# Flamingo gated block with a 2:4-sparse FFN: the down projection's weight parts are split in every step instead of read back from DRAM, and the last rows are added by VectorE

## The chip, the cores and the metric
One Trainium2 chip (trn2), one NeuronCore of it. The metric is the device time of one execution in microseconds, the median of the runs of a kernel. Lower is better.

## The reference
Inputs are x (32, 128, 512), a context of the same shape, a mask over the context's rows and two gates; the FFN's weights are w_gate and w_up (512, 2048) and w_down (2048, 512), all float32.

```python
x = x + tanh(g_xattn[0]) * xattn(layernorm(x), ctx, mask)     # softmax(q ctx^T / sqrt(512)) ctx, masked
h = silu(xn @ w_gate) * (xn @ w_up)                           # xn = layernorm(x)
h = h, with the two smaller of each four neighbours by |h| set to 0
x = x + tanh(g_ffn[0]) * (h @ w_down)
```

## The kernel before, in words
**Stages.** The first 155 us or so are attention, one batch after the other, which stores x1 to the output and the normalised x1, transposed, to a scratch tensor in DRAM (xnT). The rest is the FFN, over 4096 rows in PAIRS = 4 pairs of 1024 rows, each pair in QS = 4 quarters of the 2048 inner columns: STEPS = 16 steps `s`. A step has two units `u = 2s` and `2s + 1`, each a quarter's half of the inner columns for both halves of the pair's rows.

**Precision.** Every float32 matrix that TensorE reads is held as two fp32r parts: a high part (ScalarE copies the value to fp32r) and a low part (value less high part, by VectorE, or by POOL for w_down). A product is three matmuls: high by high, high by low, low by high.

**A unit on TensorE** (`product`, L983 to L1023): seven products (a Strassen-like form of the two-by-two block product of gate, up and the two row halves), each twice (e = 0, 1) of six matmuls, 84 in all. Product k = 4 waits for ScalarE's copy_a1 (a1_copied), k = 5 for copy_d0, k = 6 for VectorE's add_c22 (c22), k = 0 of the next unit for gated0. After the products of unit u come the down tiles of step `u // 2 - 1`, row half `u % 2` (`down`, L1069): four tiles t of 12 matmuls into two PSUM banks ps_y in turn. So half 0 of step s runs behind the products of unit 2s + 2, half 1 behind those of 2s + 3, and both halves of step 15 at the very end, with no products before them. A tile waits for the copy of the tile two before it (y_copied) and, its first, for the parts of h and of w_down.

**Hidden tiles.** For each step and row half, ScalarE makes |h| of four tiles (h_abs, in the place of h_hi), VectorE makes six compares (L849), a counting block of five instructions in bf16 (L857 to L864) and four keeps (L875); then ScalarE makes the high parts (L626) and VectorE the low parts (L882). h_abs lies over h_hi, so |h| of one half waits for the down tiles of the step before to be done.

**The down parts.** `dn` holds both parts of one quarter (2 MB over 128 partitions). Steps 0 to 3 build them: SP loads 1 MB of raw values into dn[:, 1] (L382) from a contiguous scratch copy of w_down (one 4 MB DRAM to DRAM copy, L433), ScalarE makes four high parts (L630, in unit 2s + 2, after copy_d0), POOL four low parts in place (L531), and SP stores the 2 MB to dn_scratch (L391). The quarters run to and fro (0 1 2 3, 3 2 1 0, ...), so steps 4, 8 and 12 find their parts still there; the other nine steps from 5 on reload 2 MB (L386). A load waits until the down tiles of the step before are all done, since they read the same dn.

**Weights and x.** Units 1 to 7 build their gate and up weights as units run: SP loads four raw pieces (L245), ScalarE spreads each (L261) and makes seven high parts (L273), VectorE four sums and seven low parts (L277 to L294), SP stores them (L365); later units reload them into w_ring (L372). The x parts of the next pair are made in the same way, two a unit at most, through x_blk and x_out (L311, L316 to L332, L355).

**Order of the work.** Each engine runs one list, written out by hand, and waits only at its own semaphores. On ScalarE, in the even unit: |h|, copy_a0, four h high parts, two SiLUs, two copy_a1, an x high part, spread 0, copy_d0, spread 1, copy_d0, dn high parts, w high part 0, spread 2, two h high parts, two SiLUs, w high part 1, spread 3, then the four copies of y (L640) with w high parts between them. On SP, in the odd unit of steps 0 to 2: w pieces, an x store (which waits for VectorE's x low part), w stores, the second x store, the raw load of dn, five w stores. POOL adds y to the output by accumulating DMAs (L536), four a half.

**End.** After unit 31: tiles of step 14's half 1, then ScalarE's h high parts and |h| of half 1, VectorE's h low parts, six compares, counting, keeps; the tiles of step 15's two halves; for each tile a copy by ScalarE (L640) and an adding DMA by POOL.

## Time and profile before
| | |
|---|---|
| median of 3 runs | 1163.98 us (1161.43 to 1169.27) |
| the profiled execution | 1164.87 us, its span 1163.1 us |
| TensorE matmul busy | 1091.0 us, 94% |
| VectorE, ScalarE, POOL busy | 790.7, 605.8, 230.7 us (68, 52, 20%) |
| mean granted TensorE clock | 0.982 |
| HBM read, written | 168.82 MB, 114.29 MB |

How to read it: PE is TensorE, DVE VectorE, ACT ScalarE, POOL GpSimd, SP SyncE (it issues DMAs). Matmul durations overlap (0.39 us each at a start every 0.23), so starts say more than busy shares. A gap's cause stands behind it in brackets, with its length in us. A row with x2 or more merges instructions that follow each other; its start is the first one's.

### The profile page before, as it was taken

How to read it: one execution, taken by the hardware profiler on the slowest of the kernel's cores; microseconds unless marked ns; L12 is line 12 of the kernel's file. 1: busy time of each engine (PE TensorE's matmuls, PEld its weight loads, DVE VectorE, ACT ScalarE, POOL GpSimd, SP SyncE). 2: the span in 40 equal slices, each digit the busy share in tenths (PEclk: the TensorE clock that was granted, in tenths of full speed). 3: DMA queues.
4: the chain of work that ended last, by engine and by line, in shares of the span. 5: the costliest groups of instructions: out<-in, count | busy, mean ns of one | idle time of the engine just before them, and what ended most of it. 6: DMA issues, size and time to landing. Idle time of an engine off the chain costs nothing.

```text
span 1163.1 us, 15073 instructions
## 1 busy us (share of the span) xinstructions
PE 1091.0 (94%) x4960; PEld 888.9 (76%) x4960; DVE 790.7 (68%) x1365; ACT 605.8 (52%) x1092; POOL 230.7 (20%) x413
## 2 busy tenths in 40 slices
PE   6988888799998999999999999999999999999967
PEld 5766566587776878888888788888888888888846
DVE  6999847969697676666675667575847373747480
ACT  6988556567675444444444445444544344444432
POOL 5767300313122131111110011011011111111112
PEclk9999898999999999999999999999999999999989
DMA  7999586798989997788789877887888766778445
GB/s 261 349 382 340 189 285 222 290 344 270 323 251 296 370 304 191 190 237 257 192 261 299 279 195 199 228 270 199 270 274 255 159 161 152 230 158 221 94 109 72
DMA packets 94078, 279.92 MB, mean 241 GB/s; under 512 B 9200, under 2 KB 9200, under 8 KB 89072
## 3 DMA queue, kind: packets, MB, share of 16 engines
q1 hardware_dynamic: 75568, 245.40, 59.3%
q0 software_dynamic: 18432, 33.56, 21.6%
q8 instruction: 40, 0.66, 0.2%
q14 instruction: 38, 0.31, 0.1%
HBM read 168.82 MB, written 114.29 MB: 243 GB/s over the span
## 4 chain that ended last, share of the span: by engine, by line
PE 70%; DVE 13%; DMA 9%; issue 3%; ACT 3%; SPq 1%; POOL 1%; POOLq 0%; ACTq 0%; DVEq 0%
PE ps_y L1086 9%; PE ps_y L1088 9%; PE ps_y L1087 9%; PE ps_a L1017 8%; PE ps_a L1021 8%; PE ps_a L1019 8%; PE ps_d L1017 4%; PE ps_d L1019 4%; PE ps_d L1021 4%; DMA x_blk<-xnT_scratch 3%; PE ps_c L1021 2%; PE ps_c L1017 2%; PE ps_c L1019 2%; DMA w_raw<-in_L_ffn_w_up 2%; DVE beats L849 2%
## 5 line engine op out<-in xcount | busy, mean ns | idle before, releaser
L536 POOL DMA_DIRECT2D out_rows<-y_out x128 | 110.7, 865 | 768.9 <-ACT y_out L640 741.5
L1086 PE MATMUL ps_y<-dn,h_hi 128*128 128x512 f32 x512 | 203.6, 398 | 24.6 <-DMA dn<-dn_scratch 11.4
L1017 PE MATMUL ps_a<-xm,w_ring 128*128 128x512 f32 x512 | 203.2, 397 | 15.3 <-DVE w_ring L277 7.3
L1019 PE MATMUL ps_a<-xm,w_ring 128*128 128x512 f32 x512 | 202.4, 395 | 0.0
L1021 PE MATMUL ps_a<-xm,w_ring 128*128 128x512 f32 x512 | 202.4, 395 | 0.0
L1088 PE MATMUL ps_y<-dn,h_lo 128*128 128x512 f32 x512 | 202.0, 395 | 0.0
L1087 PE MATMUL ps_y<-dn,h_hi 128*128 128x512 f32 x512 | 201.7, 394 | 0.0
L640 ACT ACTIVATE y_out<-ps_y,ffn_gate 128x512 f32<-128x512 f32 x128 | 88.0, 688 | 199.4 <-PE ps_y L1088 199.4
L817 DVE TENSOR_TENSOR cp<-ps_c,cp 128x512 f32<-128x512 f32 x64 | 43.9, 691 | 150.7 <-PE ps_c L1021 150.7
L1086 PEld LDWEIGHTS ps_y<-dn,h_hi 128*128 128x128 f32 x512 | 97.5, 190 | 49.0 <-DMA dn<-dn_scratch 11.8
L1017 PEld LDWEIGHTS ps_a<-xm,w_ring 128*128 128x128 f32 x512 | 97.6, 191 | 38.1 <-issue 9.5
L849 DVE TENSOR_TENSOR beats<-h_abs 128x512 bf16<-128x512 f32 x192 | 120.3, 686 | 1.4 <-ACT h_abs L621 1.3
L626 ACT ACTIVATE h_hi<-hidden 128x512 fp32r<-128x512 f32 x128 | 73.3, 625 | 79.2 <-DVE hidden L875 79.2
L1021 PEld LDWEIGHTS ps_a<-xm,w_ring 128*128 128x128 f32 x512 | 97.8, 191 | 20.8
L1088 PEld LDWEIGHTS ps_y<-dn,h_lo 128*128 128x128 f32 x512 | 97.6, 191 | 21.0
L1019 PEld LDWEIGHTS ps_a<-xm,w_ring 128*128 128x128 f32 x512 | 97.8, 191 | 20.6
L1087 PEld LDWEIGHTS ps_y<-dn,h_hi 128*128 128x128 f32 x512 | 97.7, 191 | 20.5
L1017 PE MATMUL ps_d<-xm,w_ring 128*128 128x512 f32 x256 | 100.1, 391 | 1.9 <-ACT hidden L607 1.9
L1019 PE MATMUL ps_d<-xm,w_ring 128*128 128x512 f32 x256 | 99.9, 390 | 0.0
L1021 PE MATMUL ps_d<-xm,w_ring 128*128 128x512 f32 x256 | 99.7, 390 | 0.0
L882 DVE TENSOR_TENSOR h_lo<-hidden,h_hi 128x512 fp32r<-128x512 f32 x128 | 81.1, 684 | 14.0 <-ACT h_hi L626 14.0
L621 ACT ACTIVATE h_abs<-hidden 128x512 f32<-128x512 f32 x128 | 76.2, 625 | 27.6 <-DVE hidden L841 27.6
(91 smaller groups left out, 1750.5 us busy)
## 6 DMA issues: line engine op xcount, KB each, us to landing
w_ring<-w_scratch SPq DMA_DIRECT2D x147, 512.0 KB, 4.6
out_rows<-y_out POOLq DMA_DIRECT2D x128, 256.0 KB, 4.1
w_scratch<-w_ring SPq DMA_DIRECT2D x56, 512.0 KB, 8.1
xm_scratch<-x_out SPq DMA_DIRECT2D x42, 512.0 KB, 5.2
xm<-xm_scratch SPq DMA_DIRECT2D x21, 1024.0 KB, 7.0
dn<-dn_scratch SPq DMA_DIRECT2D x9, 2048.0 KB, 11.1
x_in<-in_x SPq DMA_DIRECT2D x32, 256.0 KB, 6.3
ctx_in<-in_ctx SPq DMA_DIRECT2D x32, 256.0 KB, 6.4
```

The lines of the kernel that those rows point to most:

```text
L536: nc.gpsimd.dma_start(out[RING * ((s - 1) // QS) + TILES * ORDER[order] + n % TILES], y_out[:, n % 4], accum_op=ALU.add).then_inc(y_stored ...
L621: nc.scalar.activation(h_abs[:, h, j], hidden[:, h, j], ACT.Abs).then_inc(abs_done, 1)
L626: nc.scalar.activation(h_hi[:, h, j], hidden[:, h, j], ACT.Copy).then_inc(h_hi_done, 1)
L640: nc.scalar.activation(y_out[:, n % 4], ps_y[n % 2][:], ACT.Identity, scale=ffn_gate[:]).then_inc(y_copied, 1)
L849: nc.vector.tensor_tensor(beats[:, PAIR[i, j]], h_abs[:, h, i], h_abs[:, h, j], ALU.is_ge).then_inc(beats_done, 1)
L882: nc.vector.tensor_tensor(h_lo[:, h, j], hidden[:, h, j], h_hi[:, h, j].bitcast(F32), ALU.subtract).then_inc(h_lo_done, 1)
L1017: nc.tensor.matmul(to, w_ring[:, k, e, 0, c], xm[:, k, 0, c], start=begins and c == 0, stop=False, skip_group_check=not begins)
L1019: nc.tensor.matmul(to, w_ring[:, k, e, 0, c], xm[:, k, 1, c], start=False, stop=False, skip_group_check=not begins)
L1021: last = nc.tensor.matmul(to, w_ring[:, k, e, 1, c], xm[:, k, 0, c], start=False, stop=c == 1, skip_group_check=not begins)
L1086: nc.tensor.matmul(to, h_hi[:, h, j, at], dn[:, 0, j], start=at_j == 0, stop=False)
L1087: nc.tensor.matmul(to, h_hi[:, h, j, at], dn[:, 1, j], start=False, stop=False)
L1088: last = nc.tensor.matmul(to, h_lo[:, h, j, at], dn[:, 0, j], start=False, stop=at_j == GROUP - 1)
```

## The change
- dn_scratch, its stores and its reloads are gone. `DN_BUILT` lists the 13 steps that split: 0 to 3 and the nine that reloaded. From step 5 on, SP loads 1 MB of raw values straight from w_down into `w_raw`, whose use for gate and up is over by then, as soon as the split before is done (it no longer waits for the down tiles); for step 15 it does so in unit 30.
- ScalarE's high parts move forward: the first before copy_a1(0), the second before copy_a1(1), the others behind it. They wait for the raw part, and to write dn for the down tiles of the step before. POOL makes the low parts of all 13 steps.
- Step 15's parts go to `dn_last`, a place over xm that is free once product 1 of unit 31 is made; ScalarE makes the high parts behind copy_a1 of unit 31.
- |h| of step 15's half 1 goes to x_blk, so it waits for no down tile; VectorE puts two of its compares ahead of half 0's low parts.
- The last half's four tiles: SP loads these rows of the output (with all earlier additions in them) into `rows`, VectorE adds gate times ps_y to them, and SP stores them plainly. The last four y copies and accumulating DMAs are gone.
- w_down's scratch copy is made in four DMAs of 1 MB, one a step. The low parts 4 to 6 of the weights built in even units move on VectorE behind the two c11 additions of the odd unit.

```diff
+LAST = STEPS - 1
+DN_BUILT = [s for s in range(STEPS) if s < QS or s % QS]
...
+        sb = Place(0)
+        dn_last = sb("dn_last", [P, 2, GROUP, D], F32R, 4)
+        rows = sb("rows", [P, TILES, D], F32, 4)
...
+        def dn_places(s, j):
+            if s < QS:
+                return dn[:, 1, j].bitcast(F32), dn[:, 0, j], dn[:, 1, j]
+            to = dn_last if s == LAST else dn
+            return w_raw[:, j // 2, j % 2], to[:, 0, j], to[:, 1, j]
+        def abs_of(s, order):
+            return x_blk if (s, order) == (LAST, 1) else h_abs[:, ORDER[order]]
...
             def load_dn(s):
-                wait(sp, y_done, 2 * TILES * s)
                 if s < QS:
-                    if s == 0:
-                        sp.wait_ge(down_copied, 16)
-                    else:
-                        sp.wait_ge(dn_stored, 16 * s)
+                    wait(sp, y_done, 2 * TILES * s)
+                    wait(sp, dn_lo_done, GROUP * s)
+                    sp.wait_ge(down_copied, 16 * (s + 1))
                     sp.dma_start(dn[:, 1].rearrange("p j n -> p (j n)").bitcast(F32), raw_dram[s]).then_inc(dn_raw_loaded, 16)
                 else:
-                    if s == DN_RELOADED[0]:
-                        sp.wait_ge(dn_stored, 16 * QS)
-                    sp.dma_start(dn[:].rearrange("p h j n -> p (h j n)").bitcast(F32), dn_dram[weights_of(2 * s) // 2]
-                                 ).then_inc(dn_loaded, 16)
+                    sp.wait_ge(spread_done, 4 * BUILT)
+                    sp.wait_ge(dn_lo_done, GROUP * DN_BUILT.index(s))
+                    sp.dma_start(w_raw[:].rearrange("p a b n -> p (a b n)"), down_view[weights_of(2 * s) // 2]
+                                 ).then_inc(dn_raw_loaded, 16)
...
-                        if half == 0 and s > 0:
-                            store_dn(s - 1)
+                        if half == 0:
+                            if s + 1 < QS:
+                                sp.wait_ge(down_copied, 16 * (s + 1))
+                                copy_down(s + 1)
...
-                        if half == 1 and (s < QS or s in DN_RELOADED):
+                        if half == 1 and s in DN_BUILT and s != LAST:
+                            load_dn(s)
+                        if half == 0 and s == LAST:
                             load_dn(s)
...
+            b = B - RING + TILES * ORDER[1]
+            sp.dma_start(rows[:], out.rearrange("b s d -> s b d")[:, b:b + TILES]).then_inc(rows_loaded, 16)
+            for t in range(TILES):
+                sp.wait_ge(y_added, t + 1)
+                sp.dma_start(out[b + t], rows[:, t]).then_inc(rows_stored, 16)
...
+            for s in range(STEPS):
+                if s in DN_BUILT and s != LAST:
+                    dn_low(s)
+                for t in range(TILES):
+                    add_y(2 * TILES * s + t)
+                if s == LAST - 1:
+                    dn_low(LAST)
+                if s != LAST:
+                    for t in range(TILES, 2 * TILES):
+                        add_y(2 * TILES * s + t)
...
+            def dn_high(s, j):
+                raw, high, low = dn_places(s, j)
+                at = DN_BUILT.index(s)
+                act.wait_ge(dn_raw_loaded, 16 * (at + 1))
+                if s == LAST:
+                    act.wait_ge(made[1], 2 * UNITS)
+                else:
+                    wait(act, y_done, 2 * TILES * s)
+                nc.scalar.activation(high, raw, ACT.Copy).then_inc(dn_hi_done, 1)
...
                 silu0(u, 0)
                 silu0(u, 1)
+                if s - 1 in DN_BUILT:
+                    dn_high(s - 1, 0)
                 copy_a1(u, 0)
+                if s - 1 in DN_BUILT:
+                    dn_high(s - 1, 1)
                 copy_a1(u, 1)
+                if s - 1 in DN_BUILT:
+                    dn_high(s - 1, 2)
+                    dn_high(s - 1, 3)
                 x_high_at(s, 0)
...
-                if 0 < s <= QS:
-                    for j in range(GROUP):
-                        dn_high(s - 1, j)
...
+            compare(s, 1, ((0, 1), (2, 3)))
             for j in kept_order(s):
                 h_low(s, 0, j)
-            compare(s, 1, ((0, 1),) + REST + ((2, 3),))
+            compare(s, 1, REST)
...
+            for t in range(TILES):
+                n = TILES * (2 * LAST + 1) + t
+                dve.wait_ge(y_done, n + 1)
+                if t == 0:
+                    dve.wait_ge(rows_loaded, 16)
+                nc.vector.scalar_tensor_tensor(rows[:, t], ps_y[n % 2][:], ffn_gate[:], rows[:, t], ALU.mult,
+                                               ALU.add).then_inc(y_added, 1)
...
-                if s < QS:
-                    pe.wait_ge(dn_lo_done, GROUP * (s + 1))
-                elif s in DN_RELOADED:
-                    pe.wait_ge(dn_loaded, 16 * (DN_RELOADED.index(s) + 1))
+                if s in DN_BUILT:
+                    pe.wait_ge(dn_lo_done, GROUP * (DN_BUILT.index(s) + 1))
+                right = dn_last if s == LAST else dn
```

## Rows read from the trace of the kernel before
**Rows 1.** The stage table, 520 to 640 us: us, engines' busy us, clock, DMA, GB/s
```profile
520.00:640.00 120.00, 120.00 (x530) 99.25 (x529) 76.89 (x126) 55.06 (x94) 13.86 (x17) 1.00 0.86 254
```

**Rows 2.** The waits of TensorE, whole span: us in total, times, longest
```profile
PE ps_y L1086 <- DMA dn<-dn_scratch: 11.4, 1, 11.4
...
PE ps_y L1086 <- POOL dn L531: 8.6, 4, 2.7
...
PE ps_y L1086 <- ACT y_out L640: 4.5, 3, 2.2
...
PE ps_d L1017 <- ACT hidden L607: 1.9, 1, 1.9
```

**Rows 3.** Timeline of TensorE in the tail: start, us, engine, line
```profile
1131.96 0.80 PE L1086 MATMUL ps_y<-dn,h_hi 128*128 128x512 f32 x1 [11.39 <-DMA dn<-dn_scratch]
...
1138.01 0.39 PE L1088 MATMUL ps_y<-dn,h_lo 128*128 128x512 f32 x1
```

**Rows 4.** Timeline of VectorE, then ScalarE and POOL, in the tail
```profile
1118.84 0.68 DVE L875 SCALAR_TENSOR_TENSOR hidden<-part,hidden 128x512 f32<-128x512 bf16 x1
...
1124.45 3.70 DVE L849 TENSOR_TENSOR beats<-h_abs 128x512 bf16<-128x512 f32 x6
...
1128.18 0.42 DVE L857 TENSOR_TENSOR part<-beats 128x512 bf16<-128x512 bf16 x1
...
1130.91 0.69 DVE L875 SCALAR_TENSOR_TENSOR hidden<-part,hidden 128x512 f32<-128x512 bf16 x1
...
1157.09 0.69 ACT L640 ACTIVATE y_out<-ps_y,ffn_gate 128x512 f32<-128x512 f32 x1 [2.03 <-PE ps_y L1088]
...
1158.07 0.86 POOL L536 DMA_DIRECT2D out_rows<-y_out  x1 [1.85 <-ACT y_out L640]
```

**Rows 5.** DMA issues: count, KB each, median us to landing; last row L416, 256 KB each
```profile
out_rows<-y_out POOLq DMA_DIRECT2D x128, 256.0 KB, 4.1
...
dn<-down_scratch SPq DMA_DIRECT2D x4, 1024.0 KB, 7.0
...
w_raw<-in_L_ffn_w_up SPq DMA_DIRECT2D x16, 512.0 KB, 7.6
...
DMA to landing us min/median/max: 2.0/5.5/9.8
```

**Rows 6.** Timelines of SyncE, ScalarE, VectorE and TensorE around step 1's splitting
```profile
271.13 0.53 SPq L382 DMA_DIRECT2D dn<-down_scratch  x1
...
276.69 1.89 SPq L245 DMA_DIRECT2D w_raw<-in_L_ffn_w_up  x2
...
274.04 1.07 ACT L601 ACTIVATE cp<-ps_a 128x512 f32<-128x512 f32 x2
...
286.14 1.14 ACT L261 ACTIVATE w_blk<-w_raw 128x512 f32<-128x512 f32 x1 [4.88 <-DMA w_raw<-in_L_ffn_w_up]
...
293.04 0.68 DVE L283 TENSOR_TENSOR w_blk<-w_blk 128x512 f32<-128x512 f32 x1
...
297.59 0.50 PE L1086 MATMUL ps_y<-dn,h_hi 128*128 128x512 f32 x1 [1.04 <-ACT y_out L640]
```

**Rows 7.** POOL's low parts and VectorE beside them, steps 1 and 2
```profile
279.26 7.19 POOL L531 TENSOR_TENSOR dn<-dn 128x512 fp32r<-128x512 f32 x4 [12.85 <-ACT dn L630]
...
280.00 1.28 DVE L823 TENSOR_TENSOR hidden<-ps_a,hidden 128x512 f32<-128x512 f32 x2
...
281.98 1.67 DVE L860 TENSOR_TENSOR beats<-beats 128x1024 bf16<-128x1024 bf16 x1
...
346.25 0.69 DVE L332 TENSOR_TENSOR x_blk<-x_blk 128x512 f32<-128x512 f32 x1
...
L531 POOL TENSOR_TENSOR dn<-dn x1: 2566/2566/2566, 345.5 to 345.5; 128x512 fp32r<-128x512 f32 x1
```

**Rows 8.** ScalarE and VectorE in unit 14, whose products begin at 578.45
```profile
585.03 1.14 ACT L611 ACTIVATE cp<-cp 128x512 f32<-128x512 f32 x2
...
591.96 1.28 DVE L823 TENSOR_TENSOR hidden<-ps_a,hidden 128x512 f32<-128x512 f32 x2
```

More of the change, by code:

```diff
@@ L89 @@
 RELOADED = [u for u in range(BUILT, UNITS) if u % BUILT]
-DN_RELOADED = [s for s in range(QS, STEPS) if s % QS]
+LAST = STEPS - 1
+DN_BUILT = [s for s in range(STEPS) if s < QS or s % QS]
 def wait(engine, semaphore, value):
@@ L526, in _, with dn_low, add_y @@
                 pool.wait_ge(x1_stored[k], 16 * (B // 4))
[L527 to L537 removed]
+            def dn_low(s):
+                for j in range(GROUP):
+                    raw, high, low = dn_places(s, j)
+                    pool.wait_ge(dn_hi_done, GROUP * DN_BUILT.index(s) + j + 1)
+                    nc.gpsimd.tensor_tensor(low, raw, high.bitcast(F32), ALU.subtract).then_inc(dn_lo_done, 1)
+            def add_y(n):
+                order = n // TILES % 2
+                pool.wait_ge(y_copied, n + 1)
+                nc.gpsimd.dma_start(out[RING * (n // (2 * TILES * QS)) + TILES * ORDER[order] + n % TILES], y_out[:, n % 4],
+                                    accum_op=ALU.add).then_inc(y_stored[n % 4], 16)
+            for s in range(STEPS):
[8 more added lines that the diff above has]
+                        add_y(2 * TILES * s + t)
         @block.scalar
@@ L678, in _ @@
                 copy_d0(u, 1)
-                if 0 < s <= QS:
-                    for j in range(GROUP):
-                        dn_high(s - 1, j)
                 if building:
@@ L716, in _ @@
                 copy_a1(u, 1)
+                if s == LAST:
+                    for j in range(GROUP):
+                        dn_high(s, j)
                 x_high_at(s, 2)
@@ L733, in _ @@
                     absolute(s, 0, j)
+                if s == LAST:
+                    for j in range(GROUP):
+                        absolute(s, 1, j)
+                    for t, tiles in enumerate(((), kept_order(s)[:1], kept_order(s)[1:], ())):
+                        copy_y(s - 1, 1, t)
+                        for j in tiles:
+                            h_high(s, 0, j)
+                    break
                 for t in range(TILES):
@@ L741, in _ @@
                         x_high_at(s, 3)
-            for j in kept_order(STEPS - 1):
-                h_high(STEPS - 1, 0, j)
-            for j in range(GROUP):
-                absolute(STEPS - 1, 1, j)
-            for t in range(TILES):
-                copy_y(STEPS - 1, 0, t)
-                h_high(STEPS - 1, 1, kept_order(STEPS - 1)[t])
-            for t in range(TILES):
-                copy_y(STEPS - 1, 1, t)
+            for t, tiles in enumerate(((), kept_order(LAST)[:1], kept_order(LAST)[1:], ())):
+                copy_y(LAST, 0, t)
+                for j in tiles:
+                    h_high(LAST, 1, j)
         @block.vector
@@ L848, in compare @@
                     wait(dve, kept_done, GROUP * hs)
-                    nc.vector.tensor_tensor(beats[:, PAIR[i, j]], h_abs[:, h, i], h_abs[:, h, j],
+                    nc.vector.tensor_tensor(beats[:, PAIR[i, j]], abs_of(s, order)[:, i], abs_of(s, order)[:, j],
                                             ALU.is_ge).then_inc(beats_done, 1)
@@ L926, in _ @@
                     w_sum(dve, u + 1, 3)
-                    for k in range(2, PROD):
+                    for k in range(2, 4):
                         w_low(dve, nc.vector, u + 1, k)
@@ L936, in _ @@
                 add_c11(u, 1)
+                if u < BUILT:
+                    for k in range(4, PROD):
+                        w_low(dve, nc.vector, u, k)
                 if s > 0:
@@ L975, in _ @@
                 h_low(s, 1, j)
+            for t in range(TILES):
+                n = TILES * (2 * LAST + 1) + t
[4 more added lines that the diff above has]
+                                               ALU.add).then_inc(y_added, 1)
         @block.tensor
```

56 lines of the change are left out of this document (26 added, 30 removed).

## The prediction

> **What bounds the kernel now.** I read the page first, then the stage table, the waits of TensorE, the timelines of one splitting step, one later step and the tail, and the landing times of the DMAs. In 520 to 640 us TensorE starts 530 matmuls in 120 us, one per 0.226 us, with no idle time and the full granted clock [rows 1]. So in the feed-forward part TensorE is the bound, and a part of the change counts only where it makes or removes a gap there. The gaps that it touches are four kinds [rows 2]: one of 11.4 us for the reload of the down parts (the last step); four for POOL's low parts of steps 0 to 3, 8.6 us together; three for y_out, 4.5 us, at tile 3 of the down tiles of steps 0 to 2; one of 1.9 us behind a late ScalarE copy. The other eight reloads of dn never hold TensorE.
>
> Below, T is the start of the products of an even unit. A unit's products are 84 matmuls (19.0 us), a half's down tiles 48 (10.9 us); product 4 is due at T+10.9, product 6 at T+16.3, the down tiles at T+19.1.
>
> **The last step, where the gain is.** Now the tiles of step 14 are issued until 1120.6, TensorE waits 11.39 us for the 2 MB reload, which may start only then, and resumes at 1131.96 at 0.43 us per matmul, half the pace; at 1138.01 it is back at 0.23 [rows 3]. That is 13 slow matmuls, 2.7 us more. After the change the parts lie in dn_last, split during unit 31, so only the hidden tiles can hold TensorE. VectorE ends its keeps at 1119.5 [rows 4], makes two compares (0.60 each, from 3.70 for six), and the first low part is ready at 1121.4: a gap of 0.8 instead of 11.4. Half 1's tiles run 1121.4 to 1132.3. Meanwhile VectorE needs three more low parts, four compares (2.4), the counting (2.7, from 1128.18 to 1130.91), four keeps (2.4): done at 1130.8. High and low parts follow at 0.6 a tile, the first at 1131.4, so the second half starts at 1132.3 without a wait and is issued by 1143.2. Before, its last tile was handed to ScalarE at 1157.09 [rows 4]; now to VectorE at 1143.4. Gain 13.7.
> After it, before: 0.69 copy, 0.86 issue on POOL at 1158.07, 4.1 us of adding DMA [rows 4, 5], end 1163.1, in all 6.0. Now: one add of 0.7, an issue of 0.5, a plain 256 KB store. Such stores took 2.0 to 9.8, median 5.5, when the queues were full [rows 5]; here nothing else is moving, so I take 2.5, range 2.0 to 4.1: 3.8 in all, gain 2.2. The rows' load (1 MB) can start when the last add of step 14 has landed, near 1126, and with about 7 us it is there by 1133, before tile 0 is due at 1135. Below nothing: an add that takes long would stop tile 2; bound 3 us. Tail: -15.9, range -12 to -17.
>
> **Steps 0 to 2.** Here ScalarE now makes high part 0 before copy_a1, and waits for the raw part. SP still issues that load behind the x store: 271.13, and 1 MB takes 7.0 (6.8 to 7.8 in four), so it lands at 278.1 [rows 5, 6]. ScalarE starts copy_a1 at 274.04 now [rows 6]. So it stands still for some 4 us, product 4 waits 3.7 us, and what is queued behind it (x high part, spread 0, copy_d0) moves: four high parts of 0.52 and the wait add up to 6.1 us. Spread 0's end releases SP's load of the w_up piece, at 276.69 now, at 282.8 then, and ScalarE stands before spread 2 until it lands, at 286.14 now, 9.4 us after its issue, because five w stores were queued ahead. Later the queue is emptier: between 5 and the median of 7.6 [rows 5] it lands at 288.0 to 290.5. From there spread 2, two high parts of h, two SiLUs, w high and spread 3 (5.3 us, at 1.1 a spread and 0.5 to 0.6 the others) lead to VectorE's w_sum, at 293.04 now, and this over w_high to the second copy_y, for which tile 3 waits until 297.59 now [rows 6]. That chain, not TensorE, sets the step; TensorE's 3.7 us and the half clock after it are hidden in the wait for y_out. On VectorE's side now three counting instructions are stretched by POOL, 1.67 in place of 0.69 [rows 7], some 3 us; they come free because POOL starts sooner, but c22 waits for copy_d0 by as much. So w_sum starts at 294.3 (VectorE's own chain) to 295.8 (290.5 and 5.3). Net for step 1: +1.3 to +2.8. The same working with issues at 203.76 and 336.77 gives +0.6 to +1.8 for step 0 and 0 to +1.7 for step 2. Together +4.1, range 0 to +6.3. Step 3's raw part lands at 405 as ScalarE comes to it; POOL starts 5 us sooner and its 0.9 us gap goes. The smaller copies of w_down cost nothing (four of 1 MB for one of 4 MB; store_dn leaves the same queue). Moving three w_low on VectorE by half a unit fits the time in which it waits for product 1. Sum +3.2.
>
> **The eight later split steps.** ScalarE's wait is nearly nil: its SiLUs end at T+7.6 (585.03 and 1.14, T = 578.45) [rows 8], the raw load goes at about T+0.3 and takes 7; in steps 7, 13 and 14 it goes far earlier. Four high parts push copy_d0 by 2.1 us, to T+12.4; product 5 wants it at T+13.6. Cost nothing; without that cover it would be what the load is late beyond 1.2 us.
> POOL is the question. Alone its subtraction takes 1.3; one took 2.57 because it started at 345.5 under x_low and x_sum, and could not begin until 346.94 [rows 7]. VectorE, running without a gap, passed from one to the other and kept POOL out though POOL had been waiting 0.7 us. In these steps POOL is ready near T+8.5, inside four h_low and six compares without a gap, so I take it that it gets in where VectorE's first operation with a PSUM input begins, c22: at T+13.5 where there is an x_sum (591.96) [rows 8]. From c22 to POOL's end is the 6.45 us of step 1 (280.0 to 286.45) [rows 7], so the low parts are ready at T+19.95: a gap of 0.9, in two steps; in the other six c22 or the gap before it comes 0.6 to 1.1 us sooner, and the parts are in time, with 0.2 each in three of them for a copy_y made late by VectorE's 3 us of counting. +2.4. In return the reload no longer stands before the x block at 639, and the 1.9 us gap at 654 [rows 2] goes. Sum +0.5, range -2 to +12.
> The Trainium skill, "SBUF — State Buffer", section "Who interferes with whom", says that a VectorE instruction with two SBUF inputs contends with a GpSimd one that reads SBUF, that the lock is exclusive and held for an instruction, and that issue order decides. The stretched rows agree; how a waiting POOL stands against a stream of VectorE no sentence there tells, and it is the first rival.
>
> **Sum.** -15.9 + 3.2 + 0.5 = -12.2. The profiled execution took 1164.87 (span 1163.1), 0.9 above the median of 1163.98, so the forecast is 1151.8 for the median.
>
> **Rivals.**
> 1. POOL wins each handover, slower than before. For it: in step 1 the three counting instructions alternate with POOL's [rows 7]; against it: 346.25. Each subtraction then puts 1.07 us (1.67 less 0.60) into VectorE's stream before c22, 4.3 in all. c22 was done at T+14.2 with x_sum, 13.6 with x_low, 13.0 without; it decides once it is later than T+16.3. Gaps 2.2 in two steps, 1.6 in three, 1.0 in three: 12.2, less 1.9, and step 3 loses 1.5 rather than gains 0.9. In steps 0 to 2 it takes the upper end, 6.3. +18.1 - 15.9 = +2.2: 1166.2.
> 2. The raw parts of steps 0 to 2 land before ScalarE wants them, and it does not stand. The splits start 5 us sooner, c22 is free of POOL, VectorE's chain is up to 1.5 us shorter in each step: -4.5 for +4.1, so 1143.2. Against it: load and SiLU both follow VectorE, 3 us apart in all three steps, and the load takes 7.
> 3. The end gives less: the rows land late or a hidden tile holds the second half, and with a gap near 3 us the clock falls again. +4: 1155.8.
>
> **How the numbers follow.** Forecast 0.52, rival 1 0.2, rival 2 0.1, rival 3 0.18. The forecast's own range is 1147 to 1158. The range 1145 to 1166 leaves out most of rival 2, half of rival 1 and little else. A measurement of this kernel tells about 1% from no change; the border is 1152.3. Faster by over 1%: half of the forecast and rival 2 and a little of 3, 0.42; slower by over 1% needs rival 1 with more, 0.05; within, 0.53.
>
> **What would show it.** Right: no wait on a dn load; a gap near 1 us at the first down tile of step 15 and the full clock there; ScalarE standing some 3 to 4 us before the first high part in steps 0 to 2, a gap at product 4, w_up issued 6 us later; POOL's four subtractions of the later steps ending near T+20 with the first stretched to 4 us or more. Wrong: gaps before product 6 (POOL broke the stream), no wait for the raw part, or a last tile handed over later than 1146 less the earlier shift.

## The result and the profile after

The changed kernel takes 1161.47 us (median of 12 runs, 1158.17 to 1163.88), the kernel before 1165.47 beside it (12 runs, 1161.43 to 1169.27): ratio 0.9964, 95% interval 0.9949 to 0.9979. So it is faster, by 0.36%; the medians are 4.0 us apart, about a third of the 12.2 us of the forecast. The profiled executions are 1 us apart in span, 1163.1 and 1162.1: the one of the changed kernel is the slowest of its 12 runs (1163.88).

The waits of TensorE in the changed kernel's profile (us in total, times, longest), for [rows 2]:

```profile
PE ps_a L1084 <- ACT cp L636: 15.2, 4, 6.9
PE ps_a L1084 <- DVE hidden L879: 13.6, 9, 2.2
...
PE ps_y L1155 <- ACT y_out L686: 3.5, 3, 1.6
...
PE ps_y L1155 <- DVE h_lo L938: 1.1, 1, 1.1
```

The 11.4 us on the reload of dn and the 8.6 us on POOL's parts are gone, as is the 1.9 us behind a late ScalarE copy. In their place stand 13.6 us on `hidden` of L879. That is c22, the addition that frees the PSUM bank of product 4 for product 6. One of these nine waits is in unit 8 (1.24 us), eight are in units 12 to 30. Three of the four waits of the first line, 11.5 us, stand before product 4 in steps 0 to 2; the fourth is at the start of the FFN, as before. The stage table for the stretch of [rows 1], 520 to 640 us:

```profile
520.00:640.00 120.00, 116.15 (x503) 95.19 (x502) 81.56 (x120) 56.81 (x100) 25.67 (x22) 0.99 0.79 233
```

It had 530 starts of matmuls and no idle time, and has 503. The timeline of TensorE there, at product 6 of unit 14:

```profile
599.68 0.47 PE L1084 MATMUL ps_a<-xm,w_ring 128*128 128x512 f32 x1 [2.22 <-DVE hidden L879]
...
600.74 0.63 PE L1086 MATMUL ps_a<-xm,w_ring 128*128 128x512 f32 x1
601.16 0.63 PE L1088 MATMUL ps_a<-xm,w_ring 128*128 128x512 f32 x1
...
603.72 0.54 PE L1088 MATMUL ps_a<-xm,w_ring 128*128 128x512 f32 x1
604.10 0.39 PE L1155 MATMUL ps_y<-dn,h_hi 128*128 128x512 f32 x1
```

Behind the gap eight matmuls start 0.43 us apart, half the pace, 1.6 us more. What came late shows on ScalarE, VectorE and POOL in the same unit (its products start at 580.95, the T of the prediction):

```profile
587.22 2.49 DVE L938 TENSOR_TENSOR h_lo<-hidden,h_hi 128x512 fp32r<-128x512 f32 x4
...
589.02 0.64 ACT L676 ACTIVATE dn<-w_raw 128x512 fp32r<-128x512 f32 x1 [0.37 <-DMA w_raw<-in_L_ffn_w_down]
...
589.63 8.09 DVE L905 TENSOR_TENSOR beats<-h_abs 128x512 bf16<-128x512 f32 x6
...
589.74 6.84 POOL L555 TENSOR_TENSOR dn<-w_raw,dn 128x512 fp32r<-128x512 f32 x4 [6.75 <-ACT dn L676]
...
598.85 1.28 DVE L879 TENSOR_TENSOR hidden<-ps_a,hidden 128x512 f32<-128x512 f32 x2
```

The six compares take 8.09 us instead of 3.70 [rows 4]. POOL's four subtractions, ready 0.1 us after the first compare started, take 6.84 where the four of the last step, with VectorE mostly idle beside them, take 5.06. They alternate with VectorE's: the first compare takes 0.69 us, the next four 1.78 each. c22 comes at T+17.9 instead of T+13.5 [rows 8], and product 6 was due at T+16.3. The sizes of the compares one by one (source view of L905, 589 to 598 us):

```profile
L905 DVE TENSOR_TENSOR beats<-h_abs x6: 678/1776/1784, 589.6 to 597.0; 128x512 bf16<-128x512 f32 x6
```

**Where the microsecond comes from.** Four stretches, cut at rows that both profiles have: up to the first gap of the FFN, 154.52 before and 156.40 after, +1.9, attention (in the profiles of the runs below, with the same attention code, this point lies anywhere from 152.9 to 156.4); from there to tile 3 of step 2 (364.46 and 364.39), -1.9; from there to the end of step 14's tiles (1120.6 and 1135.1), +14.6; from there to the end, 42.5 and 27.0, -15.5. Together -1.0 before rounding. The tail gave what was forecast, and the steps between took it back.

### The profile page after: what moved, and what is told of

Its sections match the earlier page's. It is cut to its first block, busy times and chain, and to the rows that moved or that the text cites. A ratio compares the mean times of both kernels' runs of the same rounds, so it can differ in the third digit from the quotient of the medians.

```text
span 1162.1 us, 15204 instructions
## 1 busy us (share of the span) xinstructions
PE 1093.2 (94%) x4960; PEld 889.3 (77%) x4960; DVE 822.3 (71%) x1369; ACT 619.5 (53%) x1124; POOL 285.0 (25%) x445
## 4 chain that ended last, share of the span: by engine, by line
PE 64%; DVE 18%; DMA 8%; issue 5%; ACT 3%; SPq 1%; POOL 0%; DVEq 0%; ACTq 0%; POOLq 0%
PE ps_y L1155 8%; PE ps_y L1157 8%; PE ps_y L1156 8%; PE ps_a L1084 8%; PE ps_a L1086 7%; PE ps_a L1088 7%; DVE beats L905 5%; PE ps_d L1088 3%; PE ps_d L1086 3%; PE ps_d L1084 3%; PE ps_c L1088 2%; PE ps_c L1086 2%; PE ps_c L1084 2%; DMA x_blk<-xnT_scratch 2%; DMA dn<-down_scratch 2%
## 5 line engine op out<-in xcount | busy, mean ns | idle before, releaser
L560 POOL DMA_DIRECT2D out_rows<-y_out x124 | 107.4, 866 | 655.4 <-ACT y_out L686 629.5
L1084 PE MATMUL ps_a<-xm,w_ring 128*128 128x512 f32 x512 | 206.3, 403 | 35.1 <-ACT cp L636 15.2
L1086 PE MATMUL ps_a<-xm,w_ring 128*128 128x512 f32 x512 | 204.9, 400 | 0.0
L1088 PE MATMUL ps_a<-xm,w_ring 128*128 128x512 f32 x512 | 204.4, 399 | 0.0
L1155 PE MATMUL ps_y<-dn,h_hi 128*128 128x512 f32 x480 | 187.5, 391 | 3.5 <-ACT y_out L686 3.5
L1157 PE MATMUL ps_y<-dn,h_lo 128*128 128x512 f32 x480 | 187.2, 390 | 0.0
L1156 PE MATMUL ps_y<-dn,h_hi 128*128 128x512 f32 x480 | 186.7, 389 | 0.0
L686 ACT ACTIVATE y_out<-ps_y,ffn_gate 128x512 f32<-128x512 f32 x124 | 85.1, 687 | 165.3 <-PE ps_y L1157 165.2
L905 DVE TENSOR_TENSOR beats<-h_abs 128x512 bf16<-128x512 f32 x186 | 156.2, 897 | 1.5 <-ACT h_abs L659 1.5
L1084 PEld LDWEIGHTS ps_a<-xm,w_ring 128*128 128x128 f32 x512 | 98.8, 193 | 61.9 <-issue 33.9
L1088 PEld LDWEIGHTS ps_a<-xm,w_ring 128*128 128x128 f32 x512 | 99.3, 194 | 21.6
L1086 PEld LDWEIGHTS ps_a<-xm,w_ring 128*128 128x128 f32 x512 | 99.1, 194 | 20.7
L1155 PEld LDWEIGHTS ps_y<-dn,h_hi 128*128 128x128 f32 x480 | 90.2, 188 | 23.4 <-ACT y_out L686 4.7
L1157 PEld LDWEIGHTS ps_y<-dn,h_lo 128*128 128x128 f32 x480 | 90.1, 188 | 19.3
L1156 PEld LDWEIGHTS ps_y<-dn,h_hi 128*128 128x128 f32 x480 | 90.1, 188 | 19.1
L879 DVE TENSOR_TENSOR hidden<-ps_a,hidden 128x512 f32<-128x512 f32 x64 | 42.9, 686 | 58.9 <-PE ps_a L1088 56.9
```

The costliest lines, as they stand in the source:

```text
L560: nc.gpsimd.dma_start(out[RING * (n // (2 * TILES * QS)) + TILES * ORDER[order] + n % TILES], y_out[:, n % 4], accum_op=ALU.add).then_inc( ...
L686: nc.scalar.activation(y_out[:, n % 4], ps_y[n % 2][:], ACT.Identity, scale=ffn_gate[:]).then_inc(y_copied, 1)
L905: nc.vector.tensor_tensor(beats[:, PAIR[i, j]], abs_of(s, order)[:, i], abs_of(s, order)[:, j], ALU.is_ge).then_inc(beats_done, 1)
L1084: nc.tensor.matmul(to, w_ring[:, k, e, 0, c], xm[:, k, 0, c], start=begins and c == 0, stop=False, skip_group_check=not begins)
L1086: nc.tensor.matmul(to, w_ring[:, k, e, 0, c], xm[:, k, 1, c], start=False, stop=False, skip_group_check=not begins)
L1088: last = nc.tensor.matmul(to, w_ring[:, k, e, 1, c], xm[:, k, 0, c], start=False, stop=c == 1, skip_group_check=not begins)
```

## The experiments

Each run has its own runs of the kernel before beside it: 1164.88 us in runs 1 to 4, 1165.62 in 5 to 8, 1166.77 in 9 to 12. The ratios are to these.

**1. The tail alone.** Steps 5 to 14 store and reload both parts as before; steps 0 to 3 split early as changed.

```diff
-DN_BUILT = [s for s in range(STEPS) if s < QS or s % QS]
+DN_BUILT = [0, 1, 2, 3, LAST]
+DN_RELOADED = [s for s in range(QS, LAST) if s % QS]
...
+                        if half == 0 and s > 0:
+                            store_dn(s - 1)
```

> The changed kernel, but steps 5 to 14 reload both parts from a DRAM copy as before (the copy and its stores are back); the first steps, step 15 and the end are as changed. Theory (POOL's subtractions, reading SBUF, break VectorE's stream before c22 and so hold product 6): no gap at product 6 in the later steps, the 1.9 us gap at 654 is back, and the time is 12.4 us of gaps and some 2 of half clock below the changed kernel, so near 1147 to 1149. Rival (the end gave less than its 15.6 us, and the later steps cost little): the time stays within 3 us of the changed kernel, near 1160.

1156.87 us, ratio 0.9935 (0.9914 to 0.9956). The gaps at product 6 of the later steps are gone, but for one of 1.4 us in unit 8, the tail is as in the changed kernel, and the 1.8 us behind a late ScalarE copy is back. It missed by 8 us or more, and its profile has them in steps 1 and 2: tile 3 of step 2 starts 217.3 us after the first gap, against 209.9 before and 208.0 after. Run 10 takes this up.

**2. POOL writes and does not read** in steps 5 to 14. The low parts' values are left out, so this is a measurement and no kernel.

```diff
-                    nc.gpsimd.tensor_tensor(low, raw, high.bitcast(F32), ALU.subtract).then_inc(dn_lo_done, 1)
+                    if QS <= s < LAST:
+                        nc.gpsimd.memset(low.bitcast(F32), 0.0).then_inc(dn_lo_done, 1)
+                    else:
+                        nc.gpsimd.tensor_tensor(low, raw, high.bitcast(F32), ALU.subtract).then_inc(dn_lo_done, 1)
```

> In steps 5 to 14 POOL fills the low parts with zeros (it writes and reads nothing; the low part of w_down is left out there), ScalarE's high parts and the loads stay. Theory (the reads of POOL and VectorE meet): VectorE's six compares take 3.7 us again instead of 8.1, no gap at product 6, near 1147. Rival A (ScalarE's four high parts make copy_d0 and so c22 late): the gaps of 1.0 to 2.2 us stay, near 1161. Rival B (any POOL work on SBUF stops VectorE): the compares stay stretched, gaps as long as the fills are.

1148.37 us, ratio 0.9856 (0.9816 to 0.9895); no gap at product 6 from step 5 on. ScalarE's four copies, SP's loads and POOL's four waits are all still there. What is gone is POOL's reading, and with it some length: a fill takes 0.53 us, a subtraction 1.3. Run 11 takes these two apart.

**3. VectorE makes the low parts of steps 5 to 14**, behind c22.

```diff
+                if s - 1 >= QS and s - 1 in DN_BUILT:
+                    for j in range(GROUP):
+                        raw, high, low = dn_places(s - 1, j)
+                        dve.wait_ge(dn_hi_done, GROUP * DN_BUILT.index(s - 1) + j + 1)
+                        nc.vector.tensor_tensor(low, raw, high.bitcast(F32), ALU.subtract).then_inc(dn_lo_done, 1)
```

> In steps 5 to 14 VectorE makes the four low parts itself, behind the two c22 additions, 4 times 0.6 us. Theory: compares at 3.7 us, c22 in time, low parts ready 2.4 us after c22 at T+17.2 (due T+19.1), so no gap at product 6 nor at the first down tile, at most 0.3 us at a later tile: near 1147. Rival A (ScalarE late): gaps at product 6 stay, near 1161. Rival C (VectorE has no 2.4 us to give behind c22): gaps move to tile 2 of the down tiles, 1 to 2 us in eight steps, near 1158.

1146.66 us, ratio 0.9845 (0.9804 to 0.9886), and one gap, of 0.5 us, between unit 8 and the tail. With 2.5 us of work more on VectorE in each of eight steps the kernel is some 15 us faster than with that work on POOL.

**4. The same splits, half a step earlier**: raw load in the even unit, high parts ahead of the unit's SiLUs, POOL's subtractions in VectorE's idle time.

```diff
-                        if half == 1 and s in DN_BUILT and s != LAST:
+                        if half == 1 and s < QS:
                             load_dn(s)
-                        if half == 0 and s == LAST:
+                        if half == 0 and s > QS and s in DN_BUILT:
                             load_dn(s)
...
+                        if t == 2 * TILES - 1 and QS <= s + 1 < LAST and s + 1 in DN_BUILT:
+                            dn_low(s + 1)
```

> In steps 5 to 14 the raw part is loaded half a step earlier, ScalarE makes the four high parts first thing in the even unit and POOL starts at about T+1.5 while VectorE waits for product 1; POOL still subtracts. Theory: POOL's four take 1.3 us each and end near T+6.8, only the last one meets VectorE's low parts of h, no gap at product 6: near 1147. Rival A (ScalarE's 2.1 us make its chain late wherever they stand): copy_a0 late by 2, gaps at product 2 or 6 in each of the eight steps, 1158 or more.

1147.00 us, ratio 0.9841 (0.9793 to 0.9889). Its stage table shows TensorE full again, as [rows 1], with VectorE as busy as there (77.0 us for 76.9; 81.6 in the changed kernel):

```profile
520.00:640.00 120.00, 120.00 (x530) 99.18 (x529) 77.01 (x126) 58.38 (x103) 23.85 (x24) 1.00 0.84 245
```

**5. High parts of steps 0 to 3 at their old place**, all else as changed.

```diff
-                if s - 1 in DN_BUILT:
+                if s - 1 in DN_BUILT and s > QS:
                     dn_high(s - 1, 0)
...
+                if 0 < s <= QS:
+                    for j in range(GROUP):
+                        dn_high(s - 1, j)
```

> The changed kernel with the high parts of steps 0 to 3 put back behind the copies of product 3, where the kernel before had them; steps 5 to 14 stay as changed. Theory 1 (the one on record, that the early place costs time because ScalarE stands before the copies of product 2 until the raw rows have landed): the gaps of 6.91, 2.32 and 2.29 us at product 4 go (11.5 us), those of the kernel before at the first down tile come back (2.32, 2.67, 2.68 and about 0.9, together 8.6 us), and the copies' own 3.5 us of the first step stays: the time falls by 0 to 4 us, best value 1159. Theory 2 (the two places are worth the same within a microsecond, because the time that the early place takes from the copies it gives back at the first down tile): 1161 to 1162, and step 2's last tile starts within 1 us of 364.4 us less the shift of the start. The eight gaps at product 6 stay in both, 12.4 us together.

1160.25 us, ratio 0.9946 (0.9925 to 0.9967); the changed kernel's 0.9949 to 0.9979 overlaps. From the first gap to tile 3 of step 2 it takes 207.9 us, the changed kernel 208.0. Theory 2: the place is worth nothing that these runs resolve. Of the 11.5 us of gaps before product 4, 2.9 stay; the gaps at the down tiles of steps 0 to 2 grow from 3.5 to 11.6.

**6 and 12. POOL kept out until c22**, once by a wait for the second of the two additions (run 6, below), once for the first (run 12, `c22_done[0]`). Run 6 was meant to wait for the first, and its expectation says so, but `c22_done[1]` counts the second; run 12 is what that expectation describes.

```diff
             def dn_low(s):
+                if QS <= s < LAST:
+                    pool.wait_ge(c22_done[1], 2 * (s + 1) + 1)
```

> The changed kernel with one wait more: in steps 5 to 14 POOL begins its four subtractions only when VectorE has done the first addition of product 4's results, so that it cannot enter VectorE's unbroken run of compares. This is the order that the prediction on record took for granted. Theory 1 (POOL's reads of SBUF inside that run make product 6 late): the gaps at product 6 go (12.4 us) with the half clock behind two of them (some 3.5 us), gaps of at most about 1 us at the first down tile take their place in the five steps whose stream has an x_sum; 1146 to 1152 us, best value 1149. Theory 2 (the gaps come from ScalarE's four copies ahead of product 2's copies): the gaps stay as they are, 1161 us.

> As the run in which POOL waits for product 4's additions, but for the first of the two instead of the second: POOL may start some 0.64 us sooner, where the prediction let it in. That run had gaps of 1.63 (six) and 2.4 us (two) at the first down tile, 14.7 together, as POOL's four subtractions took 6.2 us against VectorE's counting. Theory (the end of POOL's four, not their start's neighbour, sets the gap): each gap shrinks by 0.6, 9.7 us together, and the run takes 1159.5, range 1157 to 1162. By the prediction on record the gaps would be 0.9 in two steps and nil in the others, 1151 us.

Run 6: 1164.48 us, ratio 0.9999 (0.9979 to 1.0019). Run 12: 1151.70 us, ratio 0.9883 (0.9854 to 0.9912). I had expected 1146 to 1152 of run 6 and 1157 to 1162 of run 12; it was the other way round. TensorE's waits, run 6, then run 12:

```profile
PE ps_a L1086 <- ACT cp L638: 15.3, 4, 6.8
PE ps_y L1157 <- POOL dn L557: 14.7, 8, 2.5
```

```profile
PE ps_y L1157 <- POOL dn L557: 3.0, 5, 0.9
...
PE ps_a L1086 <- DVE hidden L881: 1.4, 1, 1.4
```

In both, the eight gaps at product 6 are gone and others stand at the first down tile, 14.7 us or 3.0. The timelines of unit 14 say why (run 6, then run 12):

```profile
592.77 1.28 DVE L881 TENSOR_TENSOR hidden<-ps_a,hidden 128x512 f32<-128x512 f32 x2
...
594.14 6.19 POOL L557 TENSOR_TENSOR dn<-w_raw,dn 128x512 fp32r<-128x512 f32 x4 [13.39 <-DVE hidden L881]
...
600.38 0.50 PE L1157 MATMUL ps_y<-dn,h_hi 128*128 128x512 f32 x1 [2.42 <-POOL dn L557]
```

```profile
585.71 3.70 DVE L907 TENSOR_TENSOR beats<-h_abs 128x512 bf16<-128x512 f32 x6
...
590.53 1.29 DVE L881 TENSOR_TENSOR hidden<-ps_a,hidden 128x512 f32<-128x512 f32 x2
...
591.30 5.83 POOL L557 TENSOR_TENSOR dn<-w_raw,dn 128x512 fp32r<-128x512 f32 x4 [12.22 <-DVE hidden L881]
...
597.19 0.50 PE L1157 MATMUL ps_y<-dn,h_hi 128*128 128x512 f32 x1 [0.93 <-POOL dn L557]
```

Run 12's POOL begins under the second addition, which reads one of its inputs from PSUM and is not stretched, and its last subtraction ends 6.60 us after c22 began. Run 6's begins 1.37 us after c22 began instead of 0.77, meets four counting instructions that are stretched in full instead of three, and ends 7.56 after it. With the tiles due 5.2 to 5.7 us after c22 begins, that is a gap of 2.4 or of 0.9. In the six other steps the parts are in time or up to 0.5 us late in run 12, and 1.6 late in run 6.

**7. The last rows as in the kernel before**, by ScalarE's copy and POOL's adding DMA.

```diff
-            for t in range(TILES):
-                n = TILES * (2 * LAST + 1) + t
-                dve.wait_ge(y_done, n + 1)
-                if t == 0:
-                    dve.wait_ge(rows_loaded, 16)
-                nc.vector.scalar_tensor_tensor(rows[:, t], ps_y[n % 2][:], ffn_gate[:], rows[:, t], ALU.mult,
-                                               ALU.add).then_inc(y_added, 1)
+            for t in range(TILES):
+                copy_y(LAST, 1, t)
```

> The changed kernel with the last four row tiles written as in the kernel before: ScalarE scales them out of PSUM into y_out and POOL adds each to the output by an accumulating DMA; VectorE's four adds, the load of 1 MB and the plain stores are left out. The step of the prediction that stands to be tested: the end behind TensorE's last matmul was to become 2.2 us shorter, by 0.9 us that is the fall from a landing of 4.1 to one of about 2.0 us and the rest from the missing hop through POOL. By it this run takes 1163.5 us. Rival: the end is set elsewhere and the run takes 1161.5 us, the same.

1164.12 us, ratio 0.9989 (0.9971 to 1.0007), 2.65 above the changed kernel. The intervals of the two overlap, but their profiles bear it out: from the first matmul of the last tiles to the end of the span it takes 28.88 us, the changed kernel 25.93.

This run's profile shows one thing more. In unit 12 there is no gap at product 6, where the changed kernel has 1.63 us. POOL's first subtraction came there during the third compare instead of the first, and was kept out of all the rest:

```profile
526.02 3.70 DVE L896 TENSOR_TENSOR beats<-h_abs 128x512 bf16<-128x512 f32 x6
...
527.61 7.94 POOL L545 TENSOR_TENSOR dn<-w_raw,dn 128x512 fp32r<-128x512 f32 x4 [8.22 <-ACT dn L665]
```

That first subtraction takes 3.27 us, and the six compares their 3.70. With the same instructions, c22 is in time when POOL does not get in between.

**8. Runs 4 and 5 together**, the splits of steps 5 to 14 early and the high parts of steps 0 to 3 late.

```diff
+                if s - 1 >= QS and s - 1 in DN_BUILT:
+                    for j in range(GROUP):
+                        dn_high(s - 1, j)
                 silu0(u, 0)
...
                 copy_d0(u, 1)
+                if 0 < s <= QS:
+                    for j in range(GROUP):
+                        dn_high(s - 1, j)
```

> The kernel in which the splits of steps 5 to 14 are made in the step before, ahead of VectorE's run (147.0 us over a thousand in the last series), with the high parts of steps 0 to 3 at the place of the kernel before. If the two act apart from each other: 1147.0 us less what the first run of this series gains over the changed kernel, so 1144 to 1147, best value 1145. If the gaps in steps 0 to 3 hide something of each other it does not fall below 1147.

1145.47 us, ratio 0.983 (0.9802 to 0.9859), the best value of the expectation. Since run 5's own gain of 1.2 us is within the noise, and so are the 1.5 us to run 4, this does not show that the two act apart from each other. It is the lowest of the kernels that leave nothing out, though runs 3, 4 and 9 can't be told from it.

**9. All low parts on VectorE**, with the high parts of steps 0 to 3 late.

```diff
+                if 0 < s <= QS:
+                    for j in range(GROUP):
+                        raw, high, low = dn_places(s - 1, j)
+                        dve.wait_ge(dn_hi_done, GROUP * DN_BUILT.index(s - 1) + j + 1)
+                        nc.vector.tensor_tensor(low, raw, high.bitcast(F32), ALU.subtract).then_inc(dn_lo_done, 1)
                 add_c12(u, 0)
```

> All subtractions of steps 0 to 14 on VectorE: those of steps 5 to 14 behind the additions of product 4, as in the run that took 1146.66 us, those of steps 0 to 3 behind the first two keeps, with the high parts of steps 0 to 3 at the place of the kernel before. In the run with early and late parts the first down tiles of steps 0 to 3 still waited 2.68, 1.46, 2.55 and 1.12 us for POOL (7.8 us). If POOL and VectorE hinder each other there too, VectorE's counting loses its stretch (some 3 us a step), the four subtractions cost it 2.5 us, and those gaps go: 1138 to 1143 us, best value 1141. If VectorE's own chain up to the sums for the next weights sets these steps anyway, as the gaps at tile 3 say, nothing is gained: 1145 to 1147.

1146.04 us, ratio 0.9836 (0.9809 to 0.9864): nothing gained. The counting is unstretched, but the low parts come after it, and the gaps at the down tiles are 3.47, 2.50, 3.85 and 1.86 us, 11.7 in all where run 8 has 7.8, while those for y_out fall from 5.4 to 0.7.

**10. As run 1, with the high parts of steps 0 to 3 at their old place.**

```diff
-                if s - 1 in DN_BUILT:
-                    dn_high(s - 1, 0)
                 copy_a1(u, 0)
...
                 copy_d0(u, 1)
+                if 0 < s <= QS:
+                    for j in range(GROUP):
+                        dn_high(s - 1, j)
```

> The tail of the change alone (reload from the scratch copy in steps 5 to 14, as before), with the high parts of steps 0 to 3 back at their old place. The run of the tail alone, with the high parts early, took 1156.87 us: its last tile of step 2 started 217.3 us after the first product's gap, where the kernel before has 209.9. Theory: the early place costs these 7 us, and only because the 2 MB store stands in SP's queue ahead of what ScalarE then waits for. By it this run takes 1149.5 us, range 1147 to 1151, and no gap over 4 us stands in 200 to 400. Rival: the order of SP's queue alone costs them: 1156 to 1158, as that run.

1157.09 us, ratio 0.9918 (0.9889 to 0.9946): the same as run 1, the rival. So the early place is not what slows steps 1 and 2. ScalarE's waits for the w_up piece, 200 to 400 us, in run 10, in the kernel before, in the changed kernel and in run 5:

```profile
ACT w_blk L279 <- DMA w_raw<-in_L_ffn_w_up: 31.5, 5, 9.1
```

```profile
ACT w_blk L261 <- DMA w_raw<-in_L_ffn_w_up: 24.2, 5, 5.3
```

```profile
ACT w_blk L276 <- DMA w_raw<-in_L_ffn_w_up: 12.1, 5, 3.6
```

```profile
ACT w_blk L276 <- DMA w_raw<-in_L_ffn_w_up: 20.4, 5, 5.5
```

The median landing of these pieces in that stretch is 9.3, 8.8, 5.4 and 8.6 us after the issue. It goes with the place of the high parts and not with the 2 MB store: late in run 5, without the store, it is 8.6; early in run 1, with the store, it is 5.1.

The store does cost time here. In these steps run 10 differs from run 5, and run 1 from the changed kernel, by the 2 MB store of the parts and by the raw load that waits for it. From the first gap to tile 3 of step 2 run 10 takes 216.8 us for run 5's 207.9, and run 1 217.3 for 208.0: 9 us both times. The kernel before has the store too and takes 209.9, but makes its copy of w_down earlier, in one DMA. In run 10 store and copy stand next to each other:

```profile
225.74 0.47 SPq L415 DMA_DIRECT2D dn_scratch<-dn  x1
226.25 0.56 SPq L394 DMA_DIRECT2D down_scratch<-in_L_ffn_w_down  x1
```

and the copy lands in a median of 12.8 us, for 7.8 in the changed kernel. That it is this neighbourhood that costs the 9 us fits, and was not tested by itself.

**11. POOL copies the raw part, one input instead of two**, in steps 5 to 14. The low parts' values are left out here too.

```diff
-                        nc.gpsimd.memset(low.bitcast(F32), 0.0).then_inc(dn_lo_done, 1)
+                        nc.gpsimd.tensor_copy(low, raw).then_inc(dn_lo_done, 1)
```

> The changed kernel, but in steps 5 to 14 POOL copies the raw part to the place of the low part, with one SBUF input instead of two; the low part's value is left out. The run that only wrote there took 1148.37 us and had no gap at product 6. If any read of SBUF by POOL breaks VectorE's run, the gaps at product 6 stay, of 1.0 to 2.2 us in eight steps, shorter only as far as POOL's instruction is: 1156 to 1162 us, best value 1160. If only an instruction with two inputs on both sides does, they go: 1146 to 1149 us. This bears on the mechanism, not on a repair.

1146.01 us, ratio 0.9834 (0.9802 to 0.9866), no gap at product 6. That is not because nothing was stretched. Compares and copies of unit 14 in its timeline, and the compares one by one:

```profile
586.06 5.35 DVE L908 TENSOR_TENSOR beats<-h_abs 128x512 bf16<-128x512 f32 x6
...
586.51 0.71 POOL L556 CAST dn<-w_raw 128x512 fp32r<-128x512 f32 x1 [7.08 <-ACT dn L679]
...
587.51 0.72 POOL L556 CAST dn<-w_raw 128x512 fp32r<-128x512 f32 x1 [0.30 <-ACT dn L679]
```

```profile
L908 DVE TENSOR_TENSOR beats<-h_abs x6: 678/1093/1096, 586.1 to 590.7; 128x512 bf16<-128x512 f32 x6
```

Each of the four copies puts 0.41 us into the run of compares, 1.65 in all, against 1.1 us for each subtraction. c22 still comes in time. So my two theories were put wrongly: reading one input does hinder, by less for the shorter instruction (0.41 us for 0.71, 1.1 for 1.3), and here that stays under the slack.

## Why the prediction was wrong

**The tail: right.** Forecast -15.9, measured -15.5. Its steps in the timeline of the changed kernel:

```profile
1134.11 1.30 DVE L905 TENSOR_TENSOR beats<-x_blk 128x512 bf16<-128x512 f32 x2
...
1136.15 0.47 PE L1155 MATMUL ps_y<-dn_last,h_hi 128*128 128x512 f32 x1 [1.09 <-DVE h_lo L938]
...
1140.65 0.38 SPq L490 DMA_DIRECT2D rows<-out_rows  x1
...
1145.40 2.56 DVE L938 TENSOR_TENSOR h_lo<-hidden,h_hi 128x512 fp32r<-128x512 f32 x4
...
1150.42 0.75 DVE L1041 SCALAR_TENSOR_TENSOR rows<-ps_y,ffn_gate,rows 128x512 f32<-128x512 f32 x1 [2.46 <-PE ps_y L1157]
```

The gap is 1.09 (forecast 0.8) with the clock at full after it, the second half waits for nothing, and the rows, issued at 1140.65 with a landing of 7.1, are there before the first add. The last add is at 1158.82 and the plain stores land in 2.0 us. Run 7 prices the end at 2.65 (medians) to 2.95 us (profiles); the forecast was 2.2. Rival 3 is out.

**Steps 0 to 2: the delay was right, its price wrong.** Forecast +4.1, measured -1.9 from the FFN's first gap; 1.0 of that lies before product 0 of unit 2 (191.21 and 192.04), where nothing is split yet. In step 1 ScalarE stands 3.93 us for the raw part, forecast 4, and w_up is issued at 282.38. Unit 4 begins at 264.37 in the kernel before and at 265.51 here, so that is T+16.9, where the forecast's 282.8 was T+18.4. And the piece is there at 286.59, 4.2 us after its issue, where the forecast took 5.2 to 7.7:

```profile
277.64 0.63 ACT L676 ACTIVATE dn<-dn 128x512 fp32r<-128x512 f32 x1 [3.93 <-DMA dn<-down_scratch]
...
282.38 1.91 SPq L250 DMA_DIRECT2D w_raw<-in_L_ffn_w_up  x2
...
286.59 1.15 ACT L276 ACTIVATE w_blk<-w_raw 128x512 f32<-128x512 f32 x1 [1.71 <-DMA w_raw<-in_L_ffn_w_up]
```

The term mis-sized is the landing. "Later the queue is emptier" was right in direction and too small: w_up lands in a median of 5.4 us with the high parts early and 8.6 with them late (run 5), and ScalarE's waits for it fall from 20.4 to 12.1 us. What the early place takes before product 4 it gives back later in the step, 208.0 against 207.9 us up to tile 3 of step 2. The 2.0 us between run 5 and the kernel before are not the early place; the missing store, the smaller copies and the three moved w_low are all in them, and no run parts them. "The smaller copies of w_down cost nothing" holds only because the store goes: with both, runs 1 and 10 lose 9 us. Rival 2, that the raw parts land in time, is out.

**The later split steps: the step that failed.** It is "I take it that it gets in where VectorE's first operation with a PSUM input begins, c22". The sum had +2.4 for it, with -1.9 for the stall that goes. The stall went; the measured gaps are 1.63, 2.22, 1.62, 1.62, 2.22, 1.02, 1.02 and 1.02, 12.4 us, the figures of rival 1 to a few hundredths. Some 1.6 us of half pace come on top. And each gap costs about 0.27 us more than its idle time, as the starts show:

```profile
535.18 0.39 PE L1088 MATMUL ps_d<-xm,w_ring 128*128 128x512 f32 x1
537.20 0.47 PE L1084 MATMUL ps_a<-xm,w_ring 128*128 128x512 f32 x1 [1.63 <-DVE hidden L879]
537.51 0.39 PE L1086 MATMUL ps_a<-xm,w_ring 128*128 128x512 f32 x1
```

The starts are 2.02 us apart, 1.79 more than the usual 0.23 for a gap of 1.63, and the next start comes after 0.31. For eight gaps that is 2.2 us. Together 16.2, and between product 6 of unit 8 and the first tile of the last step lie 720.8 us here and 704.7 in run 11, 16.1 less: nothing is left to assign.

The evidence for the failed step was better than one row, and still misled. In all three of steps 0 to 2 of the kernel before, POOL's first subtraction came under the last compare or just behind it and was kept out until c22 (it took 2.45, 1.98 and 2.57 us); the row at 345.5 [rows 7] waited through two changes of instruction, not one. The stretched counting instructions of the same groups were changes that POOL won. What I did not look at is where in the run of compares POOL arrives. In the later steps it came at about T+8.8, under the first compare or the low part before it, and got in at the next; in unit 12 of run 7 it came under the third, and there the assumption held. In step 3 the 0.92 us gap at the down tile turned into 1.24 at product 6, as rival 1 has it, where the forecast gained 0.9.

**The same step, made true.** Run 12 enforces what the prediction assumed, POOL in at c22. The prediction then says low parts at T+19.95; unit 14 begins at 577.03 there, and POOL's end at 597.13 is T+20.1. It says gaps of 0.9 in two steps: measured 0.93 twice. Its 0.2 in three more were to come from a late copy_y; what is there is 0.34, 0.35 and 0.49 of waiting for POOL. That the time, 1151.7, is the forecast's 1151.8 is partly luck: against the runs beside it the gain is 13.6 us by the ratio and not 12.2, and steps 0 to 2 were better than forecast. So one premise failed, and the working behind it held for these steps. Run 6 shows how little lies between: 0.6 us later at the entry, and the kernel is back at the time of before.

**Rival 1** had the mechanism for these eight steps, and their gaps. Its total of 1166.2 was off by two errors of opposite sign: it took the upper end of 6.3 us for steps 0 to 2, and left out the 3.8 us that come on top of the gaps; with the -1.9 measured and those it would have said 1162. It was given 0.2. The mechanism is shown by runs 2, 3 and 4, which take away POOL's reads, its part, or its place in VectorE's run, and each gain 13 to 15 us on the changed kernel.

## What to carry to other kernels

When work is put on POOL because POOL is idle, price it by what VectorE is doing at that moment: each of POOL's subtractions of 1.3 us put 1.1 us into an unbroken run of VectorE's two-input instructions, and how much that run may grow is read from what follows it (in unit 14 c22 had 2.2 us to spare and came 4.4 later). A few instructions more on VectorE, or the same ones moved to where VectorE stands idle, cost nothing that shows in the time. And when a load goes out at another moment than in the old profile, its landing is to be priced anew: here the median fell from 8.6 to 5.4 us.

## What the runs showed of the hardware

- Between VectorE with two inputs in SBUF and POOL reading two, both outcomes occur, and in these profiles the place of arrival tells them apart. POOL's first subtraction of a step got in at the next change of instruction in all 32 cases in which it came under the last h_low ahead of the compares (15) or under the first or second compare (17); from there on compares started 1.7 us apart instead of 0.6. In all 21 cases in which it came under the third to fifth compare it was kept out of the compares that were left; 20 of them are in steps 0 to 2 of the profiles with early high parts, one is unit 12 of run 7. Why is open: this is what was seen, and no run moved POOL's arrival to test it.
- POOL writing without reading did not hinder: with the fills of run 2 the mean compare over the whole run is 709 ns, and 709 also in run 3, where POOL makes no low part in these steps; it is 897 in the changed kernel. (The kernel before has 686, since POOL does not stand beside the compares of step 3 there.) By the Trainium skill, "SBUF — State Buffer", section "Who interferes with whom", a two-input VectorE instruction contends with a GpSimd one that reads SBUF, not with one that only writes; the trace agrees with 709 against 897 ns. In run 11 one read is enough to hinder, and a copy of 0.71 us costs a compare 0.41.
- An addition of c22's, with one input in PSUM, is not stretched by POOL running beside it (1.29 us for the two in run 12, 1.28 in [rows 8]), which is what run 12 lives on.
- A gap of 2.22 us was followed by eight matmuls at 0.43 us in one of the two units that have it (the mean granted clock of 598 to 608 us is 0.83), and by none in the other (846 to 856 us: 1.00). In run 5, with the same gaps, both were followed by it, in run 7 only the second. No gap of 1.0 to 1.6 us in the changed kernel was followed by any.
